# A transformer block with routed experts: the loop over heads goes batch by batch, with V, norms and routing placed inside it

## What is computed

```python
x = x + layernorm(attn(layernorm(x)))
x = x + layernorm(moe(layernorm(x)))

# attn: 16 heads of 64, causal, T = 1024
logits = (q @ k.T + causal + pos_bias) / 64     # bias by distance, clipped at 127
out = softmax(logits) @ v
return concat_heads(out) @ Wo + bo

# moe: 8 experts, top 2, and a shared one; 128 -> 512 -> 128
shared = gelu(x @ Wfc_s + bfc_s) @ Wproj_s + bproj_s
probs = softmax(x @ Wr); gate = top-2 of probs, divided by their sum
routed = sum over e of (gelu(x @ Wfc[e] + bfc[e]) @ Wproj[e] + bproj[e]) * gate[:, e]
return shared + routed
```

## Time and profile before

| | |
|---|---|
| median of three runs | 845.37 us |
| the profiled execution | 844.46 us, of which its span is 842.7 us |
| mean granted TensorE clock | 0.975 |
| TensorE busy | 771.5 us, 92% of the span |
| VectorE busy | 707.7 us, 84% |
| ScalarE busy | 612.8 us, 73% |
| POOL busy | 298.9 us, 35% |
| chain of work that ended last | TensorE 75%, VectorE 8%, issue 6%, POOL 4%, ScalarE 3%, DMA 3% |

### The profile page before, as it was taken

The page is one execution under the profiler, slowest core; times in us unless marked ns, Lnnn a source line. Parts: engine busy times, 40 slices in busy tenths (PEclk is TensorE's granted clock), DMA queues, the critical chain, the costliest instruction groups (busy, mean ns, idle before and its releaser), DMA issues.

```text
span 842.7 us, 17198 instructions
## 1 busy us (share of the span) xinstructions
PE 771.5 (92%) x4436; PEld 657.1 (78%) x4436; DVE 707.7 (84%) x1596; ACT 612.8 (73%) x1340; POOL 298.9 (35%) x323
## 2 busy tenths in 40 slices
PE   3877999999999999999999999996489999999992
PEld 2656988888888888888889888885377777777771
DVE  5557888988888888888888888888778888898976
ACT  2356888887888888888788888873577767667672
POOL 2318823333332332333233233223503354445423
PEclk9899999999999999999999999999679999999997
DMA  7684334424423432442443343230003211122101
GB/s 279 219 280 89 75 66 97 88 62 87 100 62 76 95 77 62 93 94 62 87 95 67 70 97 82 62 75 26 25 1 129 76 60 43 46 75 75 51 1 50
DMA packets 56025, 70.72 MB, mean 84 GB/s; under 512 B 36032, under 2 KB 45120, under 8 KB 52544
## 3 DMA queue, kind: packets, MB, share of 16 engines
q1 hardware_dynamic: 55712, 69.83, 32.9%
q10 hardware_dynamic: 288, 0.59, 0.3%
...
## 4 chain that ended last, share of the span: by engine, by line
PE 75%; DVE 8%; issue 6%; POOL 4%; ACT 3%; DMA 3%; POOLq 0%; DVEq 0%; ACTq 0%; SPq 0%
PE out_ps L1191 16%; PE score_ps L1158 16%; PE trans_ps L1173 15%; PE shared_ps L1205 6%; PE trans_ps L1074 3%; PE score_ps L1074 3%; PE score_ps L1076 2%; PE score_ps L1075 2%; PE trans_ps L1075 2%; PE trans_ps L1076 2%; DVE pT_lo L961 2%; PE shared_ps L1074 2%; PE shared_ps L1076 2%; PE shared_ps L1075 2%; POOL rstd L421 1%
## 5 line engine op out<-in xcount | busy, mean ns | idle before, releaser
L649 ACT ACTIVATE probs<-score_ps,row_min 128x128 f32<-128x128 f32 (+7 forms) x256 | 189.9, 742 | 53.5 <-DVE row_min L848 53.4
L861 DVE TENSOR_TENSOR pT_lo<-trans_ps,pT_hi 128x512 fp32r<-128x512 f32 (+3 forms) x384 | 201.6, 552 | 16.7 <-ACT pT_hi L670 16.6
L670 ACT ACTIVATE pT_hi<-trans_ps 128x512 fp32r<-128x512 f32 (+3 forms) x384 | 185.1, 491 | 40.4 <-PE trans_ps L1173 28.8
L848 DVE CUSTOM_DVE_ANT_0 score_ps<-score_ps,bias 128x128 f32<-128x128 f32 (+7 forms) x256 | 194.6, 760 | 22.8 <-PE score_ps L1158 19.4
L1173 PE MATMUL trans_ps<-ident,probs 128*128 128x128 f32 x1152 | 190.0, 274 | 3.2 <-DVE pT_lo L861 1.8
L1158 PE MATMUL score_ps<-k_hl,q_hl 128*128 128x512 f32 (+2 forms) x768 | 182.5, 351 | 3.1 <-DMA k_hl<-k_hl 1.6
L470 POOL TENSOR_TENSOR acc<-acc,head_out 128x512 f32<-128x512 f32 x64 | 83.0, 1297 | 245.5 <-DVE head_out L879 245.3
L1173 PEld LDWEIGHTS trans_ps<-ident,probs 128*128 128x128 f32 x1152 | 136.8, 140 | 27.3 <-DVE pT_lo L861 11.9
L1191 PE MATMUL out_ps<-pT_hi,v_hl 128*128 128x512 f32 (+2 forms) x384 | 156.5, 409 | 1.1 <-DVE pT_lo L861 1.1
L961 DVE TENSOR_TENSOR pT_lo<-probs,pT_hi 128x512 fp32r<-128x512 f32 x144 | 133.2, 952 | 25.0 <-ACT pT_hi L728 15.1
L1158 PEld LDWEIGHTS score_ps<-k_hl,q_hl 128*128 128x128 f32 x768 | 134.4, 189 | 23.7 <-DMA k_hl<-k_hl 1.8
...
## 6 DMA issues: line engine op xcount, KB each, us to landing
q_hl<-k_hl SPq DMA_DIRECT2D x64, 256.0 KB, 3.6
k_hl<-k_hl SPq DMA_DIRECT2D x32, 512.0 KB, 4.2
v_scratch<-probs SPq DMA_DIRECT2D x16, 512.0 KB, 4.0
v_raw<-v_scratch SPq DMA_DIRECT2D x32, 256.0 KB, 4.6
bias_all<-gate_scratch SPq DMA_DIRECT2D x8, 1024.0 KB, 4.8
v_raw<-in_Wfc SPq DMA_DIRECT2D x8, 256.0 KB, 4.9
bias<-in_Wproj SPq DMA_DIRECT2D x8, 256.0 KB, 5.3
bias_all<-in_rel_steps SPq DMA_DIRECT2D x1, 1920.0 KB, 12.7
```

The source lines that it names most:

```text
L649: act.activation(probs[s % 4][:, 0:n], scores_of(s % QB)[:, 0:n], ACT.Exp, bias=row_min[:, s:s + 1], scale=-1.0, accum_out=row_sum[:, s:s ...
L670: act.activation(pT_hi[c][:, CH * g:CH * g + m, q * P:(q + 1) * P], trans_ps[k % 2][:, 0:m * P].rearrange("p (m q) -> p m q", q=P), ACT.Co ...
L848: dve.tensor_tensor_reduce(out=ps, in0=ps, in1=bias_b[b][:, T - n:T], scale=1.0, scalar=3e38, op0=ALU.add, op1=ALU.min, accum_out=row_min[ ...
L861: dve.tensor_tensor(pT_lo[c][dst], trans_ps[k % 2][:, 0:m * P].rearrange("p (m q) -> p m q", q=P), pT_hi[c][dst], ALU.subtract).then_inc(p ...
```

## The change

A pass of the loop now works on two heads of the same batch: passes 0 to 7 are batch 0, passes 8 to 15 batch 1, and in the tables the two halves of a pass are heads 2h' and 2h' + 1 of a batch. The number of passes, their slots and each slot's work stay. With that:

- Ahead of the loop only V of batch 0 (blocks 0 to 7) is made. V of batch 1 is made in 16 half-blocks (`later_values`) in slots 2, 4, 5, 6, 10, 12, 13, 14 of passes 1 and 2, through `shared_ps`; ScalarE copies each to `normed`, SP stores it.
- The Q/K projection of the first two halves moves ahead, behind V's block 0 and 1. The norms of chunks 2 and 3 move behind it.
- SP loads the biases of 4 heads early and those of 12 behind the last store of V, then V of head 0, then Wo, the router's weights and the layers' biases. VectorE scales the biases (two ahead of the loop, then 2, and one in each of slots 1 to 12 of pass 0), POOL masks two at a time.
- Norms of batch 0's attention output lie in slots 9 to 15 of pass 8 (VectorE) with POOL's roots in slot 11 of pass 8 and slot 0 of pass 9; the norm is applied by ScalarE in slots 2 to 5 of pass 9; transposes in its slots 10 and 12, logits in 14; the choice in slots 1 to 3 of pass 10, the turned gates in slot 4.
- Passes 0, 1, 2, 7, 8, 9, 10 and 15 are written out; 3 to 6 and 11 to 14 are two loops.
- Behind the heads come experts 0 and 1 on batch 0's two chunks, beside the norms of batch 1, then both on batch 1's. Logits are 16 columns wide instead of 256. The gates of each batch are stored and loaded by themselves.

The diff, cut to its core ("..." where lines are left out):

```diff
+    V_SLOT = {(1 + k // 8, (2, 4, 5, 6, 10, 12, 13, 14)[k % 8]): k for k in range(2 * QB)}
+    NT_SLOT = {(PAIRS + 1, 10): 0, (PAIRS + 1, 12): 1}
+    LOGIT_SLOT = (PAIRS + 1, 14)
+    GATE_SLOT = (PAIRS + 2, 4)
+    SIDE = (0, 1, 2, PAIRS - 1, PAIRS, PAIRS + 1, PAIRS + 2, H - 1)
+    STEPS = [(0, 0), (0, 1), (1, 0), (1, 1), (0, 2), (0, 3), (1, 2), (1, 3)]
...
# SP
+            sp.dma_start(bias_all[:, 0:2 * B, :], rel_steps[:, 0:2 * B, :]).then_inc(bias_loaded[0], 16)
             load_x(2)
             load_x(3)
...
+            place_q(0, 0)
+            store_v(0)
+            store_v(1)
+            place_k(0, 0)
+            for t in range(2, QB):
                 store_v(t)
...
+            sp.dma_start(bias_all[:, 2 * B:H, :], rel_steps[:, 2 * B:H, :]).then_inc(bias_loaded[1], 16)
             for r in range(4):
+                sp.wait_ge(v_stored[r], 16 * (QB // 4))
+            load_v(0, 0, 0)
+            sp.dma_start(wo[:], Wo2).then_inc(wo_loaded, 16)
+            sp.dma_start(wr[:], Wr).then_inc(small_loaded, 16)
+            sp.dma_start(layer_bias_T[:], layer_bias).then_inc(small_loaded, 16)
...
+            def store_gates(b):
+                sp.wait_ge(gate_T_ready, b + 1)
+                for j in range(CH):
+                    sp.dma_start(bass.AP(gate_dram.tensor, b * T + j * P, [[B * T, E], [W, NC], [1, P]]),
+                                 gate_T[b][j * E:(j + 1) * E, :, :]).then_inc(gates_stored, 16)
...
# POOL, behind the last pass
+            pool.wait_ge(oT_psum, H * B * NC - 1)
+            split_wfc(0, 0)
             for s in range(S, TAIL):
                 if s in WO_SLOT:
                     if WO_SLOT[s] == (B - 1, NC - 1):
+                        split_wproj(0, 0)
+                    add_head(H - 1, *WO_SLOT[s], None)
             root(1, QB, NB)
             split_wfc(1, 1)
             split_wproj(1, 1)
+            root(2, QB, NB)
...
# ScalarE
+            def later_v(k):
+                act.wait_ge(v1_psum, k + 1)
+                if k >= 4:
+                    act.wait_ge(v1_stored[k % 4], 16 * (k // 4))
+                act.activation(v_stage[k % 4], shared_ps[:], ACT.Copy).then_inc(v1_evac, 1)
...
# VectorE, in the slots
+            def beside(h, s):
+                if h == 0 and s == 0:
+                    scale_bias(2, 4)
+                    dve.wait_ge(bias_loaded[1], 16)
+                    far_bias(2 * B, H)
+                if h == 0 and 1 <= s <= 12:
+                    scale_bias(s + 3, s + 4)
+                if (static(h), s) in ((PAIRS, 9), (PAIRS, 10)):
+                    lo = CH * (s - 9)
+                    if lo == 0:
+                        dve.wait_ge(acc_added, PAIRS * B * NC)
+                    gather(acc, lo, lo + CH)
...
+                if (static(h), s) == (PAIRS, 12):
+                    start_add(0)
+                    add_normed(0, CH)
+                if (static(h), s) == (PAIRS, 13):
+                    add_normed(CH, QB)
+                if (static(h), s) in ((PAIRS, 14), (PAIRS, 15)):
+                    lo = CH * (s - 14)
+                    gather(x_sb, lo, lo + CH)
...
+                if (static(h), s) in ((PAIRS + 2, 1), (PAIRS + 2, 2)):
+                    pick_two(0, s - 1)
+                if (static(h), s) == (PAIRS + 2, 3):
+                    gates_of(0)
...
# VectorE, behind the heads
             split_hidden(0, 0)
+            start_add(1)
+            add_normed(QB, NB)
+            moments(x_sb, QB, NB)
             split_hidden(0, 1)
             gate_expert(0, 0, 0)
+            scale_and_offset(2, QB, NB)
+            split_hidden(1, 0)
+            gate_expert(0, 1, 0)
+            split_hidden(1, 1)
+            gate_expert(1, 0, 1)
+            nT_evac(1, 2, shared_ps)
+            nT_evac(1, 3, out_ps)
+            gate_expert(1, 1, 1)
             split_hidden(0, 2)
+            logits_of(1, shared_ps)
             split_hidden(0, 3)
+            pick_two(1, 0)
             gate_expert(0, 2, 0)
+            pick_two(1, 1)
+            gates_of(1)
+            split_hidden(1, 2)
+            gate_expert(0, 3, 0)
+            turn_gates(1, out_ps)
+            split_hidden(1, 3)
             for t in range(NB):
                 dve.tensor_scalar(x_sb[:, t, :], x_sb[:, t, :], shift[:, t:t + 1], None, ALU.subtract)
+            gate_expert(1, 2, 1)
...
# TensorE
+            values_of_all(0)
+            project_qk(0, 0, 0, 0)
+            values_of_all(1)
+            pe.wait_ge(qk_lo, 1)
+            pe.wait_ge(nT_ready, 2)
+            project_qk(0, 0, 1, 0)
...
# TensorE, behind the heads
+            hidden_units(0, 0, 0)
+            hidden_units(0, 1, 0)
+            second_layer(0, 0, 0)
+            pe.wait_ge(wfc_ready, 2)
+            hidden_units(1, 0, 1)
+            second_layer(0, 1, 0)
+            hidden_units(1, 1, 1)
+            second_layer(1, 0, 1)
...
+            with pe.Fori(2, NE - 2, 2) as e:
+                expert(e, 0, e - 1)
+                expert(e + 1, 1, e)
```

672 lines of the change are left out of this document (389 added, 283 removed).

## The result

The changed kernel takes 867.93 us (median of 4 runs, 867.52 to 869.65) against 844.40 for the kernel before (843.19 to 845.55, 4 runs): the ratio is 1.0281, with a 95% interval of 1.0266 to 1.0295. It is 23.5 us slower, and the time lies outside the forecast range. The profiled execution has a span of 866.2 us against 842.7.

The account below looks back on a forecast made before the run. TensorE was taken to pace the heads' loop, with VectorE having 3.6 us a pass to give. The terms -12 + 16 + 14 - 13 = +5 us on 844.46 gave 849.5 us, range 833 to 863.

Parts of the forecast that it names:

- C: Norms and routing of batch 0 in passes 8 to 10: +14 us, from +6.5, +4 and +3.5.
- TensorE paces the loop, and VectorE has 3.6 us a pass to give: Heads' loop: TensorE busy in all of 32.50 us a pass; VectorE's waits for others, 3.6 us, spread over 16 slots.
- with every wait in full: Upper case for batch 0's norms and routing in passes 8 to 10: 20 us if no wait is absorbed.
- B: V of batch 1 in passes 1 and 2: +16 us, between 11 and 20, from 11.1 of matmuls and 5.6 of waits.
- A: Ahead of the heads and head 0: -12 us, between -6 and -16, with V of batch 1 removed there.
- D: Behind the heads: -13 us, between -8 and -19; expert 2's second layer begins at 652 instead of 667.14.
- rival 1: Faster: the loop takes in batch 0's norms, which cost 4 us there; 836.5 us in all, chance 0.29.
- Rival 4: Biases land at 49 and V waits in all 16 slots, 0.4 us each: +20, 864.5 us, chance 0.15.
- Wrong if the loop grows by under 22 us: Sign against the prediction: the heads' loop growing by under 22 us in all.

Follow-up runs that it names:

- e6_spread: Changed kernel with batch 0's norms, routing and picks spread over passes 8 to 11 instead of 8 to 10, two blocks a slot instead of four: 867.66 us.
- e8_dve_twice: Changed kernel with VectorE gathering batch 0's statistics of the sum and of x twice in pass 8, same slots: 874.14 us.
- e9_act_twice: Changed kernel with ScalarE normalising each of batch 0's eight blocks twice in pass 9, once into a spare tile: 872.41 us.
- e1_gate: Changed kernel with the transposes of batch 0's gates moved from slot 4 to slot 10 of pass 10: 868.01 us.
- e4_rootlate: Changed kernel with VectorE taking POOL's root one slot later in pass 8 (13, not 12), both gathers of x in slots 14 and 15: 866.83 us.
- e2_vslots: Changed kernel with V of batch 1 in slots 4, 6, 12 and 14 of passes 1 to 4 instead of eight slots of passes 1 and 2: 861.93 us.
- e3_bias: Changed kernel with the load of the other twelve heads' biases issued right behind the last load of x: 865.74 us.
- e13_v_wide: Changed kernel with V in e2_vslots' slots, e3_bias's load, norms, routing and experts' first steps behind the last head in the earlier order, 256-column router tile: 847.10 us.
- e14_all_wide: Changed kernel with the edits of e2_vslots, e3_bias and e6_spread together, and the router's tile of 256 columns for both batches' logits: 858.98 us.

## Why the prediction was wrong

The direction was right, by way of a sum of which C was mis-sized most: +25.5 instead of +14. The other three terms were off by 1.6 to 2.8 us, all to the same side, so nothing cancelled; C alone is 11.5 of the 18.5 us.

**What bounds the loop.** "TensorE paces the loop, and VectorE has 3.6 us a pass to give" is the sentence that failed, in its second half and in the passes to which I applied it. The row of VectorE's waits is right, and spare time is what I read into it: e6_spread laid VectorE's work thin over four passes, and half a microsecond of 3.5 was taken in. TensorE's full busy time holds for a plain pass. I took it for the engine that paces in passes 8 to 10 too, where the added work made VectorE the limit in some slots and ScalarE in others; what was then added to them (e8_dve_twice, e9_act_twice) passed in full.

**C, +14 forecast, +25.5 measured.** In pass 8 I counted 7.9 us of work and 1.5 us of waiting for POOL, 9.4 us; it was 8.8 and 1.8. From that I took VectorE's 1.9 us of free time and a further part for TensorE, and passed on 6.5; 10.4 was right. In pass 9 I counted TensorE's 2 us and a wait for the bank and set VectorE's part "against slack", 3.4 us rounded up to 4; I left out ScalarE's eight normalising activations altogether, and they cost 1.6 us. In the slots with the transposes, the splits and the logits (the row minimum of slot 8 to that of the next slot 0) it takes 20.9 us where a plain half takes 16.3: 4.6 and not 3.4. The pass was +6.9. In pass 10 the picks and gates were counted at 4.2 us within slots 1 to 4; their rows sum to 5.0, with the short waits between them near 6, and the pass cost 7.5. One of these rows was held up by POOL: a 128x8 operation at 417.57 took 1.02 us and ended with POOL's addition, and the same line at 418.92 took 0.17.

```profile
417.57 1.02 DVE L1075 TENSOR_TENSOR top<-top,first 128x8 f32<-128x8 f32 x1
...
418.92 0.17 DVE L1075 TENSOR_TENSOR top<-top,first 128x8 f32<-128x8 f32 x1
...
417.31 1.26 POOL L531 TENSOR_TENSOR acc<-acc,head_out 128x512 f32<-128x512 f32 x1 [9.27 <-DVE head_out L995]
```

By the Trainium skill's rule on the shared port pair ("SBUF — State Buffer"), which the prediction named, the trace agrees here. For the additions in slots 12 and 13 of pass 8, where I had kept 2 us in the range, nothing came: they took 1.14 and 1.13 us for four each, and four of before's eight would be 1.09. POOL had next to nothing beside them (no operation from 354.02 to 358.61, and the second four end at 358.83), so they do not test the rule.

The range had a C "with every wait in full" at 20, still 5.5 short. Pass 11 adds 0.7, but it is plain in e1_gate, e4_rootlate and e9_act_twice, so that may not be the norms'. The largest part of the rest is pass 10, where 4.2 us were counted and 7.5 charged; then come ScalarE's 1.6 us in pass 9 and pass 8 (9.4 counted, 10.4 charged).

**B, +16 forecast, +18.8 measured.** The four waits of 1.4 us are there as foreseen, and worth what was said (e2_vslots: 5.9 us less in the passes, for 5.6). The 11.1 us of matmuls cost 12.2 there. The 0.7 us of TensorE's slack that I took back didn't exist (32.50 of 32.50 us busy). Another 0.5 us is the comparison: pass 1 of the kernel before was itself 0.5 us shorter than a plain pass. What is left, about 1 us over sixteen products, may be ScalarE's copies, which I counted at nothing.

**A, -12 forecast, -9.6 measured.** The load of the biases landed 7.6 us behind its issue, as taken, but its issue came 2.9 us later than my end-to-end count had it, which gave 46.94 for 43.5. My count laid VectorE's and ScalarE's copies of V tightly; the first scores came at 38.74 and not near 36. e3_bias took away the wait that I had named as the limit and got 3.3 us up to the end of pass 0.

**D, -13 forecast, -11.4 measured.** The waits of 1.7 and 3.1 us are there as 2.82 and 2.45. `gate_expert(1, 2)` did not wait for the load of the gates: it ran at 685.14, straight behind VectorE's other work. What is late in its place is POOL. TensorE's wait of 2.88 us ends at 691.64, and POOL's split of expert 2's second weights at 691.54:

```profile
686.07 3.11 POOL L627 TENSOR_TENSOR acc<-acc,head_out 128x512 f32<-128x512 f32 x1 [23.03 <-PE trans_ps L1257]
689.13 1.07 POOL L616 CAST pT_hi<-bias 128x512 fp32r<-128x512 f32 x1
690.28 1.26 POOL L618 TENSOR_TENSOR pT_lo<-bias,pT_hi 128x512 fp32r<-128x512 f32 x1
```

That POOL's split sets this end is read from the trace; no run took it away.

**The rivals.** That the loop takes the norms in at a C of 4 us (rival 1) is refuted by e6_spread. Rival 4, at 864.5, came nearest, but by another road: the biases landed at 46.5 and V waited in four slots, not in sixteen. "Wrong if the loop grows by under 22 us" did not happen; from mark 0 to mark 15 it grew by 44.2.

**Why moving the norms loses.** Behind the last head they stood where TensorE waits 11.04 and 5.13 us, and otherwise beside the experts' matmuls; taking them out gave back 11.4 us. In the loop they are charged 25.5. Taking them out again shows the balance by itself: e13_v_wide, which has V in the loop and the norms behind the last head, is 11.9 us faster than e14_all_wide, which has both in the loop (the norms spread as in e6_spread). V ahead of the heads against V in the loop is about even in its best form (e13_v_wide: mark 1 comes 11.6 us sooner, passes 1 to 4 are 13.0 us longer). No version that was run beats the kernel before.
